# Attention stage of a decoder layer: VectorE's side work placed in other quarters of a batch, the counting products in the next batch's first quarter, and the router's transpose behind the second scores

## The reference

```python
def _L0_xattn_ref(query, key_value, Wq, bq, Wk, bk, Wv, bv, Wo, bo):
    ...
    q = (query @ Wq + bq).reshape(B, Nq, H, D).transpose(0, 2, 1, 3)
    k = (key_value @ Wk + bk).reshape(B, Nkv, H, D).transpose(0, 2, 1, 3)
    v = (key_value @ Wv + bv).reshape(B, Nkv, H, D).transpose(0, 2, 1, 3)
    attn = jnp.einsum('bhqd,bhkd->bhqk', q, k) * scale
    attn = jnp.clip(attn, -CLAMP, CLAMP)
    attn = jax.nn.softmax(attn, axis=-1)
    ...
    x = jnp.einsum('bhqk,bhkd->bqhd', attn, v).reshape(B, Nq, Cq)
    return x @ Wo + bo
def _L0_ffn_ref(x, Wr, W1, W2):
    ...
    logits = flat @ Wr.T
    weights, ids = jax.lax.top_k(logits, K)
    weights = jax.nn.softmax(weights, axis=-1)
    ...
x = x + _L0_xattn_ref(_layernorm(x, axis=-1), ctx_768, ...)
x = x + _L0_ffn_ref(_layernorm(x, axis=-1), ...)
```

## Time and profile before

| what | value |
|---|---|
| median of 3 runs | 1611.56 us (1610.73 to 1614.21) |
| profiled execution, its own time | 1611.83 us |
| span of the profiled execution | 1609.9 us |
| mean granted TensorE clock | 0.953 of full |
| PE busy | 1367.0 us, 85% |
| DVE busy | 1020.0 us, 63% |
| POOL busy | 786.4 us, 49% |
| ACT busy | 553.0 us, 34% |

### The profile page before, as it was taken

The page is one execution under the profiler, slowest core; times in us unless marked ns, Lnnn a source line. Parts: engine busy times, 40 slices in busy tenths (PEclk is TensorE's granted clock), DMA queues, the critical chain, the costliest instruction groups (busy, mean ns, idle before and its releaser), DMA issues. The chain is left out here.

```text
span 1609.9 us, 31655 instructions
## 1 busy us (share of the span) xinstructions
PE 1367.0 (85%) x9914; PEld 947.0 (59%) x9915; DVE 1020.0 (63%) x2361; ACT 553.0 (34%) x1356; POOL 786.4 (49%) x1072
## 2 busy tenths in 40 slices
PE   4788778877746998999998899999986699999996
PEld 2455555545534666666666666666664366666664
DVE  2687987798741777888787888888875122222221
ACT  1333323323311345444354444444442112122221
POOL 3234643463343557766666666777664122222222
PEclk9999999999975899999899999999995799999999
DMA  4992000000005655656555564655551122222222
GB/s 148 304 321 60 1 1 1 0 0 1 1 0 92 93 85 106 117 113 107 109 103 115 109 113 96 111 117 118 112 110 38 39 45 44 46 46 46 44 45 23
DMA packets 180329, 128.01 MB, mean 80 GB/s; under 512 B 69010, under 2 KB 173090, under 8 KB 180194
## 3 DMA queue, kind: packets, MB, share of 16 engines
q1 hardware_dynamic: 167890, 112.23, 33.0%
q0 software_dynamic: 12304, 14.10, 5.8%
HBM read 36.10 MB, written 44.83 MB: 50 GB/s over the span
## 5 line engine op out<-in xcount | busy, mean ns | idle before, releaser
L1327 DVE TENSOR_REDUCE neg_raw<-bank_s 100x2 f32<-100x722 f32 x256 | 231.0, 902 | 97.4 <-PE bank_s L1536 86.5
L1220 ACT ACTIVATE prob<-bank_st 120x400 f32<-120x400 f32 (+1 forms) x384 | 166.3, 512 | 190.1 <-PE bank_st L1553 190.1
L1877 POOL DMA_INDIRECT out<-result,target x57 | 88.2, 1547 | 266.6 <-DVE result L1851 263.7
L1338 DVE TENSOR_SCALAR bank_st<-bank_st 120x400 f32<-120x400 f32 (+1 forms) x384 | 195.3, 570 | 0.2 <-issue 0.2
L748 PE MATMUL bank_l<-q_heads,k 128*100 128x192 f32 (+4 forms) x512 | 119.3, 372 | 65.4 <-DVE attn L562 52.2
L1075 POOL TENSOR_TENSOR neg_diag<-xident_b,neg_max 100x400 bf16<-100x400 bf16 x128 | 109.4, 855 | 124.7 <-DVE neg_max L1332 116.4
L1862 DVE TENSOR_TENSOR hidden<-silu,ebank_v 128x512 f32<-128x512 f32 x57 | 39.2, 688 | 196.7 <-PE ebank_v L1786 196.7
L1536 PE MATMUL bank_s<-k_st,q_st 96*100 96x361 bf16 x512 | 130.6, 337 | 35.0 <-DVE neg_raw L1327 21.4
L748 PEld LDWEIGHTS bank_l<-q_heads,k 128*100 128x100 f32 x512 | 79.0, 172 | 113.8 <-DVE attn L562 43.2
L396 ACT ACTIVATE q_heads<-q 32x192 f32<-32x192 f32 (+3 forms) x168 | 62.1, 370 | 224.4 <-DVE q L521 221.4
L1544 PEld LDWEIGHTS bank_st<-q_st,k_st 96*120 96x120 bf16 (+1 forms) x1536 | 109.9, 137 | 22.2 <-ACT prob L1220 10.9
(11 more groups left out here) (203 smaller groups left out, 2724.7 us busy)
## 6 DMA issues: line engine op xcount, KB each, us to landing
k_st<-k_part SPq DMA_DIRECT2D x384, 90.2 KB
slot_rows<-empty SPq DMA_DIRECT2D x9, 2967.0 KB, 26.3
q_st<-q_part SPq DMA_DIRECT2D x384, 25.0 KB
kv<-in_ctx_t SPq DMA_DIRECT2D x32, 270.8 KB
expert_w<-in_w SPq DMA_DIRECT2D x16, 512.0 KB, 4.1
rows<-slot_rows SPq DMA_DIRECT2D x57, 129.0 KB
residual<-in_w SPq DMA_DIRECT2D x16, 256.0 KB, 4.5
residual<-in_x SPq DMA_DIRECT2D x8, 400.0 KB
```

The costliest lines, as they stand in the source:

```text
L1220: act.activation(prob[0:KEYS[c], t % 2, c], bank_st[c][0:KEYS[c], 0:4 * T], ACT.Exp).then_inc(exp_done, 1)
L1327: dve.tensor_reduce(neg_raw[:, h:h + 2], bank_s[0:T, :, 0:S], AX.X, ALU.max, negate=True).then_inc(max_done, 1)
L1338: dve.tensor_scalar(tile, tile, CLAMP, -CLAMP, ALU.min, ALU.max).then_inc(clipped, 1)
```

## The change

It moves work within `body` of VectorE and of TensorE in `stage_attention`; it adds none and removes none. Line numbers of the kernel after are one to three lower from `body` on.

On VectorE:
- `place` goes from ahead of the first maxima of the first quarter to behind them;
- `moments` goes from the second quarter, ahead of the clips, to the first, behind the clips;
- `norm` goes from the second quarter to the third, behind the clips;
- `moments3` goes from the last quarter, ahead of the clips, to the third, behind the clips and `norm`;
- `one_hots` goes from ahead of the clips of the third quarter to behind the second maxima and the negation.

On TensorE:
- `count` goes from the end of an odd batch's last quarter to the first quarter of the next (even) batch, behind `scores_t`;
- `turn3`, with its waits, goes from ahead of `weigh` in the first quarter to behind the second scores.

```diff
             def body(b, q, i):
-                first = isinstance(b, int) and b == 0
                 p, more = q % 2, more_than(b, 1)
                 for t in range(4):
                     n = 4 * b + t
                     go = t < 3 or more
-                    if t == 0 and p == 0 and not (isinstance(b, int) and b < 4):
-                        place(2 * i - 2 + q // 2, q // 2)
-                    if t == 1 and not (isinstance(b, int) and b < 2):
+                    if t == 1 and b >= 2:
                         best_two(b - 2, p, 2 * i - 1 + q // 2)
                     if go:
                         maxima(n + 1, (t + 1) % 4, 0)
-                    if more_than(b, 2) and t == 1:
-                        moments(b + 2)
-                    if t == 2 and p == 1 and not (isinstance(b, int) and b < 3):
-                        one_hots(2 * i - 1 + q // 2)
-                    if t == 2 and not first:
+                    if t == 0 and p == 0 and b >= 4:
+                        place(2 * i - 2 + q // 2, q // 2)
+                    if t == 2 and b:
                         residual(b - 1, 1 - p)
-                    if t == 3 and not first:
-                        moments3(b - 1)
                     for c in range(3):
                         clip(n, c)
-                    if t == 1 and not first:
+                    if t == 0 and more_than(b, 2):
+                        moments(b + 2)
+                    if t == 1 and b:
                         normalise(b - 1)
-                    if more_than(b, 2) and t == 1:
+                    if t == 2 and more_than(b, 2):
                         norm(b + 2)
-                    if t == 3 and not first:
+                    if t == 2 and b:
+                        moments3(b - 1)
+                    if t == 3 and b:
                         norm3(b - 1, (q - 1) % 4, i if q else i - 1)
                     if go:
                         maxima(n + 1, (t + 1) % 4, 1)
                         negated(n + 1, (t + 1) % 4)
+                    if t == 2 and p == 1 and b >= 3:
+                        one_hots(2 * i - 1 + q // 2)
...
                     for c in range(3):
                         scores_t(n, p, t, c)
-                    if t == 0 and routed:
-                        if p == 0 and not (isinstance(b, int) and b < 4):
-                            pe.wait_ge(chosen_done, 2 * i - 1 + q // 2)
-                        if more:
-                            turn3(b - 2, (q - 2) % 4, k_done, CC * (b + 2))
-                        else:
-                            turn3(b - 2, (q - 2) % 4, x_done, BATCH - 2)
+                    if t == 0 and p == 0 and b >= 4:
+                        count(2 * i - 2 + q // 2, k_done, CC * (b + 2))
...
                     if go:
                         scores(nb, np_, nt, 1)
+                    if t == 0 and routed:
+                        if p == 0 and b >= 4:
+                            pe.wait_ge(chosen_done, 2 * i - 1 + q // 2)
+                        if more:
+                            turn3(b - 2, (q - 2) % 4, k_done, CC * (b + 2))
+                        else:
+                            turn3(b - 2, (q - 2) % 4, x_done, BATCH - 2)
...
-                    if t == 3 and p == 1 and not (isinstance(b, int) and b < 3):
-                        if more2:
-                            count(2 * i - 1 + q // 2, k_done, CC * (b + 3))
-                        else:
-                            count(2 * i - 1 + q // 2, x_done, b)
             every_batch(body)
             last = BATCH // 2 - 1
+            count(last - 1, x_done, BATCH - 1)
```

## The result

| what | before | after |
|---|---|---|
| median, 12 runs each | 1610.4 us (1605.82 to 1614.21) | 1620.72 us (1613.68 to 1626.46) |
| ratio, 95% interval | | 1.0055 [1.004, 1.0071] |
| profiled execution, own time (span) | 1611.83 (1609.9) | 1621.61 (1619.6) |
| mean granted clock of the profiled execution | 0.953 | 0.944 |
| PE / DVE / POOL busy, us | 1367.0 / 1020.0 / 786.4 | 1369.2 / 1023.8 / 783.9 |

The changed kernel is slower by 0.55%, or 9 us, where 1.6 were forecast; its median lies 0.7 us above the upper end of the stated range, 1602 to 1620. The first interval begins at 1.004, the other two end at 1.005 and 1.0044; all three lie above 1.

What follows compares the result with a forecast made beforehand. It took quarters to end by TensorE or VectorE, whichever is later, with GpSimd's splits setting last quarters. Rounds of 22.11 (even) and 21.87 (odd) average 21.99 against 21.93: +1.6 us over 28 batches, 1613.4 us, range 1602 to 1620.

Steps and rivals of the forecast that it cites:

- point forecast: Whole kernel: 1.6 us slower than the profiled 1611.8, giving 1613.4 us; chance 0.48.
- The likeliest case: Whole kernel: a time indistinguishable from no change, within about 0.2% or 3.2 us; chance 0.40.
- the case given 0.36: Whole kernel: measurably slower, by more than about 0.2% or 3.2 us.
- Third quarter, 5.17: Every batch: bound by VectorE, gains `norm` and `moments3`; next scores at 5.17 us instead of 4.69, the pause gone.
- rival 1: Third quarters of even batches: VectorE's 0.50 us pause before the second maxima stays; 1621 in full, 1617 if half; chance 0.24.
- Last quarter of an odd batch, 5.55: Counting products leave; GpSimd's splits hold `norm3`, then VectorE's maxima set the length: 5.55 us instead of 5.89.
- rival 2: Last quarters: VectorE's `norm3` gets in before GpSimd's splits and takes 0.40 us; 10 us faster, 1601; chance 0.10.
- Last quarter of an even batch, 5.80 unchanged: GpSimd's chain through scatter and splits already sets the end, so moving `moments3` gains 0.
- First quarter of an even batch, 5.29: Counting products come in, `place` and `moments` join VectorE's list; scores at 5.29 us instead of 4.80.
- Second quarter, 6.10: Every batch: `moments` and `norm` leave, the 0.35 us wait for `heads` goes; TensorE-bound, 6.10 us instead of 6.45.
- Lateness absorbed: Last quarter: some 0.7 us of lateness of the stacked queries vanishes behind the GpSimd chain that sets its end.
- rival 3: The 27.0 us slow-clock batch goes, 1608.4, or comes twice, 1618.4; headed as faster; chance 0.13.

Runs made afterwards that it cites:

- e_fill: Changed kernel plus four unused TensorE transposes in the idle ahead of the last quarter: 1609.8 us, 0.9976 of the kernel before.
- e_count: Kernel before with only the change's counting products, `turn3` and `place` moved: 1610.16 us, ratio 0.9985.
- e_before_fill: Kernel before plus four unused TensorE transposes ahead of the turning of xn: 1612.91 us, ratio 0.998.
- e_vector: Kernel before with only VectorE's moves of `moments`, `norm`, `moments3` and `one_hots`: 1626.74 us, ratio 1.0107.
- c_after2: Changed kernel measured again, unchanged, as base for the filled kernels: 1616.45 us, 1.0025 of the kernel before.
- c_after: Changed kernel measured once more, unchanged, in the first set of experiments: 1619.85 us, 1.003 of the kernel before.
- e_both: Changed kernel with GpSimd's `norm3` root ahead of `diag`, VectorE's `norm3` ahead of the last quarter's clips, `norm` back in the second: 1614.83 us, ratio 0.9991.
- e_ahead: Changed kernel with GpSimd's `norm3` root behind the first sends, VectorE's `norm3` in the third quarter, `norm` back in the second: 1610.24 us, ratio 0.9976.

## Why the prediction came out as it did

The sign of the point forecast was right and its size too small. The likeliest case was a time within 0.2% (0.40); the ratios of all three measurements are above that, in the case given 0.36, though the intervals of two reach below it. The point was 7 us off in the first and 2 to 3 in the others (1.0025 and 1.003 of 1611.6 are 1615.6 and 1616.4). The steps, one by one, on the changed kernel's profile (median lengths of quarters):

- *Third quarter, 5.17.* VectorE's second maxima end 4.97 after the quarter's scores in odd and even batches alike, which makes 5.12, with the pause of rows 5 gone. Right. Where the stacked queries land later it is longer (median 5.36 in odd batches). So rival 1 is out: the second maxima follow the list without idle.
- *Last quarter of an odd batch, 5.55.* Medians of 5.40 to 5.49 in three profiles, and 5.54 to 5.56 where nothing came late. Right, and for the named reason (VectorE, then GpSimd in order of time, one odd batch of the changed kernel):

```profile
704.94 1.79 DVE L1362 TENSOR_SCALAR row<-residual,moment 100x256 f32<-100x256 f32 x1
706.65 0.89 DVE L1327 TENSOR_REDUCE neg_raw<-bank_s 100x2 f32<-100x722 f32 x1
```

```profile
704.88 0.86 POOL L1056 TENSOR_TENSOR kr<-kf,k_part 128x361 f32<-128x361 f32 x1
705.71 0.87 POOL L1057 TENSOR_TENSOR k_part<-kf,k_part 128x361 bf16<-128x361 f32 x1
```

  `norm3` ends at 706.73, 0.15 after the second split. The first split is 0.06 ahead of it, not 0.45 as in rows 5 and 7, and that is enough; rival 2 (VectorE first) is out in the changed kernel. `norm3` takes 1682 ns at the median, not 1400:

```profile
L1362 DVE TENSOR_SCALAR row<-residual,moment x32: 403/1682/1802, 570.6 to 1245.0; 100x256 f32<-100x256 f32 x32
```

- *Last quarter of an even batch, 5.80 unchanged.* Measured 5.79. Right: `moments3` has left it and nothing came of that.
- *First quarter of an even batch, 5.29.* Measured 5.23 where all went as I had it, but 5.87 in others. The step missed an instruction of `place`. Behind the first maxima it meets GpSimd's splits (VectorE, then GpSimd):

```profile
709.49 0.19 DVE L1398 TENSOR_REDUCE slot_f<-chosen 100x4 f32<-100x32 f32 x1
709.71 0.80 DVE L1401 TENSOR_TENSOR slots<-slot_f,first_slot 100x4 uint32<-100x4 f32 x1
```

```profile
708.78 0.87 POOL L1056 TENSOR_TENSOR kr<-kf,k_part 128x361 f32<-128x361 f32 x1
709.62 0.87 POOL L1057 TENSOR_TENSOR k_part<-kf,k_part 128x361 bf16<-128x361 f32 x1
```

  The addition of two tiles of four columns takes 0.80 us instead of 0.16, and ends at 710.51, again with the split's end (710.49). Between batches it is 161 to 819 ns. An error of up to 0.64, in half of the batches or fewer (it is over 0.6 in four of the sixteen `slots`).
- *Second quarter, 6.10.* Measured 6.01 in odd and 5.77 in even batches. The `heads` wait is gone; behind the longer first quarter TensorE saves 0.3 more, and this pays for the miss above.
- *Lateness absorbed.* In time, yes: behind late queries a last quarter takes down to 4.7 us, not 5.5 to 5.8, while the third quarter is up to 1.5 longer. The round is 21.92 against 21.99 forecast.

Summed, the rounds at full clock give 0 where I had 1.6, and with the slow rounds the stage takes 1.3 us more. The sum of the work was sound; what it lacked was the clock. The **step that failed** is the one on lateness, in the words that some 0.7 of it "vanishes": it vanishes from VectorE's path, while TensorE stands idle all the same. The third quarter now leaves TensorE idle for 1.0 us in every batch, and a late landing makes that 1.5 to 2.8. Before, the same idle was split over `heads`, `kf` and the third quarter. I had the price of a low-clock round (rival 3: "It may also come twice: 1618.4"), but gave it 0.13 and took it for chance, with both signs alike. It had a sign. By the traces' clock records the stretch between the two points has 20.7, 23.9 and 22.1 us at the lower level in the three profiles of the changed kernel, 13.7 in both of the kernel before. The latter's 10.2 us round cost 27.0 - 21.9 = 5.1, so 0.5 us for each; the changed kernel's two of 6.8 us cost 2.3 and 2.7, so 0.34 and 0.4. The 7 to 10 us more then cost 2 to 5.

A second term stood at nothing without a reason: everything outside the rounds. The sum adds 1.6 to 1611.8 as if the rest of the program stayed as it was. In the profiles it did not: batch 0's last quarter starts at 546.2, 543.5 and 543.3 us in the changed kernel, at 539.3 and 539.6 in the kernel before, and the time at the lower level up to there is 96 to 106 us against 78.5 and 81.9. These 4 to 7 us are most of what separates the spans, and the instructions of the mixing stage, where most of that time passes, are the same in all kernels. Why its clock differs is open. It doesn't simply follow the kernel: e_fill has 81.9 us there, but e_count 102.4 and e_before_fill 105.8 (its last quarter of batch 0 starts at 546.0), and both of these were no slower than the kernel before. One profile of each kernel can't tell chance from cause.

What is shown and what isn't. Shown: in three measurements, 36 runs, the changed kernel is slower, without longer rounds at full clock, and at a lower mean clock in the two that have both clocks; the loss comes with VectorE's moves (one measurement, with 4 runs of e_vector), and goes when the idle at this one place is partly filled. Not shown: that the attention stage holds all of it. The mean clock is lower by 0.0036 and 0.0049 (c_after2 and c_after), which over 1615 us is about 12 and 16 us more at half the clock; the 8.4 and 10.2 us more that their profiles have in the attention stage are about two thirds of that. That it is the gathering more than the amount of idle is what e_both and e_ahead speak for: both idle less in all than the kernel before (50 and 44 us against 53), have 8 and 13 long idles against 3, and the third lowest and the lowest clock. For the change itself the two can't be told apart, since both grew (63 against 53).

## What to carry to other kernels

A wait that is "absorbed" on the path of one engine is still an idle of another. Where TensorE's rounds are tight, write down where its idles stand and how long the longest becomes, beside the sum of the work; several short waits merged into one long one can cost more than the sum saves, as e_both and e_ahead suggest. A cheap test is to fill the idle with products that nobody reads: if the kernel gets faster and its mean clock rises with more work, idle time was costing clock. Run it on the kernel before as well, since that one may gain too. And where a profile is compared with a profile, first see how much of the difference lies in stages that the change doesn't touch. And before an instruction of VectorE moves, even one on four columns, look at what GpSimd runs at its new place.

## What the runs showed of the hardware

- Between the last quarters of batch 0 and of batch 30 every fall of the clock, in all the profiles, came in an idle of TensorE of 1.3 to 2.8 us or at most 2.1 us behind one. These lengths are no threshold: near the stage's start, at 524 to 531 us, the clock fell beside idles of 1.0 us. Not every such idle has a fall: in the first profile of the changed kernel four of the nine over 1.3 us do. The count differs between the changed kernel's profiles; that this makes the spread of 1612 to 1628 us in c_after is likely by its correlation with the clock, and not shown. The Trainium skill (TensorE: Matmul & The Clock Gate, "What's actually happening") calls the lower level the default, which activity releases. The traces agree so far as adding products raised the mean clock in each of the three pairs, by 0.0037 to 0.0069 (0.9479 to 0.9516, 0.9451 to 0.9506, 0.9384 to 0.9453; the last pair on two chips, whose kernels before differ by 0.0013).
- GpSimd instructions that follow each other without a gap kept VectorE's `norm3` out through two of them. In e_both it ended only behind `diag` and the first split. Where it met the first of the two splits it ended 0.15 us after the second one every time, so that its 0.40 us took 1.0 to 1.8.
- A VectorE operation on two tiles of SBUF is held too, but through one instruction only: `slots` takes 161 to 819 ns in the changed kernel, and where it is long it ends 0.02 us after the split that was running, also where the second split follows without a gap (469 ns at 622.5). The Trainium skill (SBUF — State Buffer, "Who interferes with whom") says that a VectorE instruction with two inputs in SBUF contends with a GpSimd instruction that reads SBUF, and the trace agrees.
